# Reordering the opening of a gated cross-attention and mixture-of-experts kernel: shared scales first, first loads from ScalarE, one tile transposed ahead of the first product

## What is computed

```python
def _L0_xattn_ref(x, adj, W, b):            # x: ctx_512, adj: layernorm(x)
    si = jnp.einsum('bnd,d->bn', x, Wi[0])
    sj = jnp.einsum('bnd,d->bn', x, Wj[0])
    xij = jax.nn.sigmoid(si[:, :, None] + sj[:, None, :] + b[0])
    return P_ASEM * xij + (1.0 - P_ASEM) * adj

def _L0_ffn_ref(hidden, ...):               # 16 experts, 4 per token, and a shared one
    probs = jax.nn.softmax(x @ gate_w.T, axis=-1)
    vals, idx = jax.lax.top_k(probs, K)
    ...
    act_s = swiglu(x @ dequant_fp4(shared_gate_up_packed, shared_gate_up_scales))
    out = out + act_s @ dequant_fp4(shared_down_packed, shared_down_scales)

x = x + jnp.tanh(g_xattn[0]) * _L0_xattn_ref(ctx_512, _layernorm(x), W, b)
x = x + jnp.tanh(g_ffn[0]) * _L0_ffn_ref(_layernorm(x), ...)
```

## Time and profile before

| | |
|---|---|
| median of three timed runs | 688.72 us (688.53 to 691.19) |
| profiled execution, its time | 687.41 us |
| profiled execution, its span | 685.6 us |
| busy share PE / DVE / ACT / POOL | 92% / 71% / 47% / 48% |
| granted TensorE clock, mean | 0.982 |
| chain that ended last, PE's share | 80% (DVE 6%, DMA, ACT and POOL 3% each) |
| start of the first gate/up product | 45.4 us |

### The profile page before, as it was taken

The page is one execution under the profiler, slowest core; times in us unless marked ns, Lnnn a source line. Parts: engine busy times, 40 slices in busy tenths (PEclk is TensorE's granted clock), DMA queues, the critical chain, the costliest instruction groups (busy, mean ns, idle before and its releaser), DMA issues.

```text
span 685.6 us, 17258 instructions
## 1 busy us (share of the span) xinstructions
PE 629.7 (92%) x4394; PEld 382.1 (56%) x4395; DVE 488.1 (71%) x1271; ACT 325.3 (47%) x558; POOL 326.2 (48%) x506
## 2 busy tenths in 40 slices
PE   3768969999998999999999999999999999999992
PEld 2444536557554656565665656566565656656561
DVE  6979779895766858588888767778588878767110
ACT  1763567331343455454544554454554545455541
POOL 3621834100334465564646555464655656565432
PEclk9999989999999999999999999999999999999997
DMA  8780101128157875768587594847767587654533
GB/s 234 202 247 2 63 31 64 62 54 276 49 172 160 189 173 127 176 123 195 110 203 176 126 223 74 226 85 201 168 135 183 117 199 158 152 86 77 93 39 39
DMA packets 49841, 93.72 MB, mean 137 GB/s; under 512 B 8840, under 2 KB 16776, under 8 KB 49816
## 3 DMA queue, kind: packets, MB, share of 16 engines
q0 software_dynamic: 16128, 38.35, 30.3%
q1 hardware_dynamic: 32936, 55.04, 27.5%
q10 hardware_dynamic: 752, 0.04, 0.1%
HBM read 65.16 MB, written 28.24 MB: 136 GB/s over the span
## 4 chain that ended last, share of the span: by engine, by line
PE 80%; DVE 6%; DMA 3%; ACT 3%; POOL 3%; issue 2%; SPq 1%; DVEq 0%; POOLq 0%; ACTq 0%
PE gu_ps L1207 45%; PE bank L1235 22%; PE bank L1247 4%; PE bank L1221 4%; DMA dn_sc<-dn_scale_halves 2%; PE bank L1262 1%; DMA room_a<-in_ctx 1%; PE gu_ps L1167 1%; POOL room_a L462 1%; PE bank L1164 1%; PE bank L1191 1%; DVE stats L725 1%; POOL X L445 1%; DVE X L1000 1%; ACT mix_room L581 1%
## 5 line engine op out<-in xcount | busy, mean ns | idle before, releaser
L1207 PE MATMUL gu_ps<-wgu,mix_room 128*128 x1728 | 305.9, 327 | 2.7 <-DVE tick L950 1.6
L1207 PEld LDWEIGHTS gu_ps<-wgu,mix_room 128*128 128x128 f16 x1728 | 166.5, 98 | 114.7 <-issue 7.5
L1235 PE MATMUL bank<-wdn,aT 128*128 (+1 forms) x792 | 186.2, 380 | 3.2 <-ACT aT L629 2.6
L530 POOL DMA_INDIRECT out<-mix_room,idx_s x72 | 122.9, 1707 | 32.4 <-issue 30.9
L629 ACT ACTIVATE aT<-bank 128x768 f16<-128x768 f16 x88 | 71.2, 809 | 139.5 <-PE bank L1221 136.2
L1235 PEld LDWEIGHTS bank<-wdn,aT 128*128 128x128 f16 x792 | 77.6, 98 | 88.8 <-issue 3.6
L501 POOL TENSOR_TENSOR pool_tick<-ones 128x1 f32<-128x1 f32 x144 | 35.7, 248 | 163.6 <-DMA out<-mix_room,idx_s 84.0
L991 DVE SCALAR_TENSOR_TENSOR act<-gu_ps,wslot,sg x72 | 44.5, 618 | 96.4 <-ACT sg L615 84.8
L622 ACT ACTIVATE acth<-act 128x384 f16<-128x384 f32 x88 | 46.0, 523 | 120.1 <-DVE act L991 120.1
L512 POOL DMA_INDIRECT room_b<-token_rows,idx_g x72 | 76.0, 1055 | 12.3 <-issue 3.6
L927 DVE TENSOR_TENSOR wgu<-dq_code,gu_sc 128x768 f16<-128x768 f16 x136 | 72.5, 574 | 2.3
(11 more groups left out here) (157 smaller groups left out, 588.1 us busy)
## 6 DMA issues: line engine op xcount, KB each, us to landing
dn_sc<-dn_scale_halves SPq DMA_DIRECT2D x34, 384.0 KB
dn_raw<-in_L_ffn_down_packed SPq DMA_DIRECT2D x48, 256.0 KB
gu_sc<-gu_scale_halves SPq DMA_DIRECT2D x34, 192.0 KB
X<-in_x SPq DMA_DIRECT2D x4, 1024.0 KB, 8.4
token_rows<-room_a SPq DMA_DIRECT2D x16, 256.0 KB, 2.2
out<-X SPq DMA_DIRECT2D x4, 1024.0 KB, 11.1
gu_raw<-in_L_ffn_gate_up_packed SPq DMA_DIRECT2D x16, 192.0 KB
gu_raw<-in_L_ffn_gate_up_packed SPq DMA_DIRECT2D x16, 191.9 KB
```

The costliest lines, as they stand in the source:

```text
L530: nc.gpsimd.indirect_dma_start(out[:, :], bass.IndirectOffsetOnAxis(idx_s[:, b:b + 1], 0), y_sb[:, b, :], None, compute_op=ALU.add).then_i ...
L1207: mm = nc.tensor.matmul(ps[b][:, 0:I], x(xp * HC + c), wgu[:, w, wp, c, col:col + I], start=(c == 0 and xp == 0 and wp == 0), stop=(c == H ...
L1235: mm = nc.tensor.matmul(y_ps[0 if shared else b][:, :], aT[:, b, ap, t, :], wdn[:, w, wp, t, :], start=(n == 0), stop=(n == 3 * IC - 1))
```

## The change

The split of the scales is done in two parts: the 36 columns of the shared expert first, the 576 of the routed ones after slot 2. ACT issues the contexts and the first X, ahead of and behind the small constants. SP loads the shared scales and the shared packed words first, then the rest. DVE does the gates ahead of `first_stats(0)`, dequantizes the shared gate/up weights from right behind `x_factors(0)` on, and does `first_stats(1)` behind them and `x_factors(1)` behind the first down quarter. PE transposes one tile, not four, ahead of the first product, and tiles 1 to 3 between the products of slots 0 to 2; tile 4 goes behind the second half of slot 3. ACT's copies follow that order. POOL's list is the same as before. The diff's core:

```diff
@@ -144,3 +144,3 @@
         SC_SH, SD_SH = G_GU * GU // P, IC * H // P
-        sc_cut = [0, SC_SH, SC_SH * NE, SC_SH * NE + SD_SH, (SC_SH + SD_SH) * NE]
+        sc_cut = [0, SC_SH, SC_SH + SD_SH, SC_SH * NE + SD_SH, (SC_SH + SD_SH) * NE]
         SCW = sc_cut[-1]
@@ -150,3 +150,3 @@
         sc_rest = sc_room[:, 4 * SCW:6 * SCW].bitcast(F32)
-        sc_h = sc_room[:, 4 * SCW:6 * SCW].rearrange("p (a n) -> p a n", a=2)
+        sc_h = sc_room[:, 6 * SCW:8 * SCW].rearrange("p (a n) -> p a n", a=2)
...
@@ -324,5 +343,7 @@
-        def loaded(n):
+        FIRST_LOADS = 4
-            return 16 * LOADS * (n // 2 + 1)
+        def loaded(n, buf):
+
+            return 16 * LOADS * (n // 2 + 1) - (16 * FIRST_LOADS if buf == 0 else 0)
...
@@ -344,7 +364,4 @@
                 return ap.rearrange("(p n) -> p n", n=sc_cut[k + 1] - sc_cut[k])
-            for k, ap in enumerate((sh_gu_scales.rearrange("g n -> (g n)"), gu_scales.rearrange("e g n -> (e g n)"),
-                                    sh_dn_scales.rearrange("g n -> (g n)"), dn_scales.rearrange("e g n -> (e g n)"))):
-                sp.dma_start(sc_all[:, columns(k)], spread(ap, k)).then_inc(ld_sc, 16)
-            def load_ctx(b):
-                sp.dma_start(ctxs[:, b * TB:(b + 1) * TB, :], ctx_t[b]).then_inc(ld_ctx[b], 16)
+            def load_scale_columns(k, ap, landed):
+                sp.dma_start(sc_all[:, columns(k)], spread(ap, k)).then_inc(landed, 16)
...
-            load_ctx(0)
-            load_x(0)
-            for b in range(1, B):
-                load_ctx(b)
-            load_x(1)
-            sp.wait_ge(vs, SPLIT_STEPS)
-            for part, done in ((0, st_sc_sh), (1, st_sc)):
-                for k, dram in ((part, gu_s_dram), (2 + part, dn_s_dram)):
+            def store_scale_halves(part, done):
...
@@ -364,13 +375,4 @@
                         sp.dma_start(spread(flat, k), sc_h[:, hl, columns(k)]).then_inc(done, 16)
-                if part == 0:
-                    load_words(sp, sh_gu_packed, sh_dn_packed, 0)
-            sp.wait_ge(st_sc_sh, 64)
-            load_scales(sp, 0, 0)
-            sp.wait_ge(ld_w[0], 16 * LOADS)
-            for b in range(2, B):
-                load_x(b)
-            load_words(sp, gu_packed[0], dn_packed[0], 1)
-            sp.wait_ge(st_sc, 64)
-            load_scales(sp, 1, 1)
-            for i in range(NT):
+
...
+            load_scale_columns(0, sh_gu_scales.rearrange("g n -> (g n)"), ld_sc_sh)
+            load_scale_columns(1, sh_dn_scales.rearrange("g n -> (g n)"), ld_sc_sh)
+            load_gate_words(sp, sh_gu_packed, 0, ld_first)
+            sp.wait_ge(split_ready, 1)
+            store_scale_halves(0, st_sc_sh)
+            sp.wait_ge(st_sc_sh, 64)
+            load_gate_scales(sp, 0, 0, ld_first)
+            load_down_words(sp, sh_dn_packed, 0)
+            load_down_scales(sp, 0, 0)
+            load_x(1)
+            load_scale_columns(2, gu_scales.rearrange("e g n -> (e g n)"), ld_sc)
+            load_scale_columns(3, dn_scales.rearrange("e g n -> (e g n)"), ld_sc)
+            for b in range(2, B):
+                load_x(b)
+            load_words(sp, gu_packed[0], dn_packed[0], 1)
+            for i in range(TB):
+                store_rows(i)
+            sp.wait_ge(split_ready, 2)
+            store_scale_halves(1, st_sc)
+            sp.wait_ge(st_sc, 64)
+            load_scales(sp, 1, 1)
+            for i in range(TB, NT):
+                store_rows(i)
...
@@ -549,2 +574,6 @@
         def _(a):
+            def load_ctx(b):
+                a.dma_start(ctxs[:, b * TB:(b + 1) * TB, :], ctx_t[b]).then_inc(ld_ctx[b], 16)
+            load_ctx(0)
+            a.dma_start(X[:, 0:TB, :], x_t[0]).then_inc(ld_x[0], 16)
             for k in range(2):
@@ -556,2 +585,4 @@
             a.dma_start(gws[:, :], gate_w).then_inc(ld_const, 16)
+            for b in range(1, B):
+                load_ctx(b)
@@ -587,7 +618,10 @@
-            for b in range(B - 1):
-                copy_ctxT(b)
+            copy_ctxT(0)
+            copy_ctxT(1)
             scores(0)
-            copy_ctxT(B - 1)
+            copy_ctxT(2)
             scores(1)
+            copy_ctxT(3)
+            scores(2)
+            scores(3)
             for hl in range(2):
@@ -598,9 +632,8 @@
                                      ACT.Copy).then_inc(gwT_ready, 1)
-            scores(2)
-            scores(3)
-            for i in range(TB):
-                high_x(i)
-                if i:
-                    copy_xT(i - 1)
-            copy_xT(TB - 1)
+            high_x(0)
+            high_x(1)
+            copy_xT(0)
+            high_x(2)
+            copy_xT(1)
+            high_x(3)
@@ -648,4 +681,5 @@
-            for i in range(2):
-                activate(i, i)
+            activate(0, 0)
+            copy_xT(2)
+            activate(1, 1)
             copy_aT(0, 0)
@@ -653,2 +687,4 @@
                 copy_aT(i - 1, (i - 1) % 2)
+                if i == 2:
+                    copy_xT(3)
                 if i in WITH_X:
...
-            v.wait_ge(ld_sc, 64)
-            step(nc.vector.tensor_scalar(sc_top, sc_all, SPLITTER, None, ALU.mult))
-            step(nc.vector.tensor_tensor(sc_rest, sc_top, sc_all, ALU.subtract))
...
+            def split_scales(at):
+
+                step(nc.vector.tensor_scalar(sc_top[:, at], sc_all[:, at], SPLITTER, None, ALU.mult))
...
+                nc.vector.scalar_tensor_tensor(sc_h[:, 1, at], sc_all[:, at], W_SCALE, sc_h[:, 0, at], ALU.mult,
+                                               ALU.subtract).then_inc(split_ready, 1)
+            v.wait_ge(ld_sc_sh, 32)
+            split_scales(slice(0, sc_cut[2]))
             v.wait_ge(ld_const, 16 * 6)
@@ -942,3 +981,6 @@
                     v.wait_ge(dqs, n * N_STEPS + 1 - D_STEPS - 1)
-                v.wait_ge(ld_w[buf], loaded(n))
+                if isinstance(n, int) and n == 0:
+                    v.wait_ge(ld_first, 16 * FIRST_LOADS)
+                else:
+                    v.wait_ge(ld_w[buf], loaded(n, buf))
                 words = gu_raw[:, buf, :].bitcast(U16).rearrange("p (n f) -> p n f", f=2)
@@ -968,10 +1010,10 @@
+            split_gates()
             first_stats(0)
             row_scores(0)
-            split_gates()
             x_factors(0)
-            first_stats(1)
+            take_words(0, 0)
+            dequant(0, 0, 0, None)
             row_scores(1)
             attend(0)
-            x_factors(1)
             row_scores(2)
@@ -979,4 +1021,3 @@
             row_scores(3)
-            take_words(0, 0)
-            for k in range(PARTS):
+            for k in range(1, PARTS):
                 dequant(0, 0, k, None)
@@ -984,2 +1025,3 @@
             nc.vector.memset(tick[:, 0:1], 0.0).then_inc(dqg_ready, 1)
+            first_stats(1)
@@ -1005,2 +1047,3 @@
                 if k == 0:
+                    take_words(1, 1)
                     dequant(1, 1, 0, None)
@@ -1035,2 +1078,4 @@
                 if i == 2:
+                    v.wait_ge(ld_sc, 32)
+                    split_scales(slice(sc_cut[2], SCW))
                     first_stats(2)
@@ -1073,2 +1118,3 @@
+            v.wait_ge(ld_w[0], loaded(0, 0))
             for d in range(PARTS):
@@ -1076,2 +1122,4 @@
                     dequant(0, 0, None, d)
+                    if d == 0:
+                        x_factors(1)
                 else:
@@ -1082,3 +1130,2 @@
             nc.vector.memset(tick[:, 0:1], 0.0).then_inc(dq_ready, 1)
-            take_words(1, 1)
             attend(1)
@@ -1168,3 +1215,2 @@
             transpose_ctx(0)
-            transpose_ctx(1)
             pe.wait_ge(wj_ready, 1)
@@ -1172,7 +1218,5 @@
             score_parts(0)
-            transpose_ctx(2)
-            score_parts(1)
-            transpose_ctx(3)
-            score_parts(2)
-            score_parts(3)
+            for b in range(1, B):
+                transpose_ctx(b)
+                score_parts(b)
@@ -1266,2 +1310,4 @@
             def shared_gate_up(i, half):
+                if half == 0:
+                    pe.wait_ge(xT_ready, i + 1)
                 gate_up(i, i % 2, lambda k: xT[:, i, k // HC, k % HC, :], 0, half)
@@ -1270,12 +1316,13 @@
             pe.wait_ge(si_ready, B)
-            for i in range(TB):
-                transpose_x(i)
-                if i:
-                    route(i - 1)
+            transpose_x(0)
             pe.wait_ge(sig_ready, NT)
             pe.wait_ge(dqg_ready, 1)
-            for i in range(2):
-                for half in range(2):
-                    shared_gate_up(i, half)
-            route(TB - 1)
+            shared_gate_up(0, 0)
+            transpose_x(1)
+            route(0)
+            shared_gate_up(0, 1)
+            shared_gate_up(1, 0)
+            transpose_x(2)
+            route(1)
+            shared_gate_up(1, 1)
             transpose_act(0, 0)
@@ -1290,5 +1337,8 @@
                 transpose_act(i - 1, 1 - b)
-                if i in WITH_X:
```

(8 more changed lines are left out.)

29 lines of the change are left out of this document (20 added, 9 removed).

## The result

The changed kernel takes 705.14 us (median of 4 runs, 705.09 to 709.09) against 689.69 us (688.53 to 691.19, 4 runs) of the kernel before on the same chip: a ratio of 1.0237 with a 95% interval of 1.0194 to 1.028. The forecast was 699.3 with a range of 694.5 to 703.5. The sign and the chain of causes were right; the size was some 6 us short, and the measured time lies 1.6 us above the upper end of the range. Between the two medians lie 15.5 us.

What follows compares the result with a forecast made beforehand. Bound: PE, through its first product at 45.44 and 10.3 us idle after it. Delays of 7.5 (first product), 9.8 (gate), 9.3 (attend(1)), then 10.6 (tile 8): 687.4 + 10.6 = 698.0, plus 1.3 gives 699.3 us; range 694.5 to 703.5.

Steps and rivals of the forecast that it cites:

- rival (a): Between first product and tile 8, products put ahead of transposes hand back about 4 us: 695.3 us; chance 0.14.
- (c): Stores of rows 4 to 7 come later than high_x(8) needs them, some 4 us more: 703.3 us; chance 0.04.
- some 10: Behind the 576-column split: some 10 us for issues and landing of its halves, ahead of a 4.8 us load, all hidden.
- loads ahead of the first dequantization: SyncE's packed words and shared scales in the opening: cost nothing, hidden by 7 us of DVE work.
- first product, put at 2.4 us: First 12 matmuls on PE, ahead of the first gate: 2.4 us, half of 4.80.
- the same steps as before: First gate to attend(1): unchanged except take_words(1,1) moved to slot 5, 0.5 us back, so the delay is 9.3 us.
- a split of 3.3 us: DVE's 576-column split in slot 2: 3.3 us, 2.0 of it in idle time, so 1.3 added and 10.6 in all.
- the list products, put at nothing: PE's list products behind tile 8: no further delay, 10.6 us there as at tile 8.
- 2.0 us set for sharing with POOL's scaled_x: DVE's part 0 of the first dequantization, slowed beside POOL's four scaled_x: 2.0 us, with 0 to 3 as bounds.
- Rival (b): In the opening, constants or shared scales come late, at the upper bound of 12.5: 3 us more, 702.3 us; chance 0.15.
- Rival (d): POOL's second group does not hold up the first tile; first product at 36.7, run ends near 683 us; chance 0.04.
- The outer sum: Slow end: constants at 12.5, all 3.0 us lost beside scaled_x, and the low clock (up to 1.5 us): 704.8 us.

Runs made afterwards that it cites:

- pool_order: Changed kernel with only POOL's list reordered, group 0's second norm and low_x(0) to low_x(2) ahead of group 1's inverse_std: 689.31 us, ratio 1.0006.
- stats_ahead: Changed kernel with first_stats(1) and x_factors(1) moved on DVE ahead of parts 1 to 3 of the first dequantization: 697.58 us, ratio 1.0108.
- warm2: Changed kernel with 270 identity transposes added on PE in its idle time ahead of tile 0: 703.1 us, ratio 1.0204.
- list_dense: Changed kernel with one identity transpose behind each of the 62 list matmuls not last in their block: 703.5 us, ratio 1.0225.
- the experiment on the list products: Both kernels profiled again unchanged (707.45 and 690.72 us), and both with transposes put between list matmuls (703.5 and 689.87 us).
- warm: Changed kernel with 320 identity transposes added on PE in its idle time ahead of tile 0: 702.86 us, ratio 1.0197.

## Why the prediction was right in sign and short in size

**What held.** The bound, the order of the chain, and what each wait of it up to the first gate ended on. PE sets the pace from tile 8 on, so what delays tile 8 goes into the end. POOL's order decides the first product (53.92 for a forecast of 53.0, pool_order and stats_ahead from both sides). The first gate hangs on ACT with the table load right ahead of it (60.49, then 61.78). Between gate and tile 8 nothing is handed back on balance (46.4 us for 42.2), so rival (a) is out, and high_x(8) did not wait for its row, so (c) is out. dqg_ready came at 37.67 for 36.5, x_factors(1) ended at 43.1 for 42.2. The "some 10" for the issues and the landing of the split halves was too much: behind the second split the loads were issued 3.0 us after the first store (85.31 to 88.30), so that this way was hidden with more to spare than said.

**What failed, in short.** Not the order of events but the terms of the sum. The loads ahead of the first dequantization, put at nothing, cost a wait of 2.73 us. The first product, put at 2.4 us, took 3.63 at the low clock. The way from attend(1) to tile 8, put at "the same steps as before" and a split of 3.3 us, had a slow down product and a split of 5.76 us beside POOL. And the list products, put at nothing, ran 3.7 us longer at a lower clock.

**What failed, in the order of the sum.** The forecast said 10.6 us; the span shows 17.7. The 7.1 us between them are these terms:

1. Loads costed at nothing. "I cost its loads at nothing, hidden by the 7 us of DVE work" was wrong: take_words(0,0) waits 2.73 us for gu_sc, whose load took 6.8 us from its issue at 13.23. The 2.0 us set for sharing with POOL's scaled_x were then not needed, since that had ended by 20.45; with x_factors(0) 0.6 late (the constants at 10.27 for 9.55, as late as in the second profile of the kernel before) part 0 ended 1.5 late, dqg_ready 1.2 and the first product 0.9. That the first product came so near its forecast is therefore in part luck: 2.73 us of waiting that were not in the sum and 2.0 us of sharing that were in it and not needed. The prediction named 1 to 3 us "without that cover"; the cover was there on paper, 7 us, and was too short.
2. The first twelve matmuls taken at 2.4 us, "half of 4.80", from a row in which PE had been at work and the clock was 1.00. They took 3.63: 1.2 us. With item 1 that is 2.1; the steps behind it gave 0.4 back (tile 1's transposes took 0.5 for the 0.8 put down), so that the gate is 1.7 late against the forecast. The clock was left out of the sum although the change took 7.9 us of PE work out of the opening and so gave PE the 20.8 us of idle time behind which the clock was low.
3. "attend(1) follows by the same steps as before ... nothing is handed back" held for attend(1) (11.1 against 9.3, all of it carried over), but not for the slots behind it: from there to low(2) 2.1 us more were lost, where the first down product ran 3.04 us and DVE waited 0.68 and 0.72 us for products and 0.57 for an activation. warm2, with these products at full clock, takes 1.7 of it back. Since list_dense has them at full clock without a fill, this loss may belong to the execution and not to the change; both profiles of the changed kernel show it.
4. The split costed at 3.3 us, "3.5 times 576/612", from a row with nothing beside it. In slot 2 it took 5.76 beside POOL's low_x: 2.5 us more. Where it met one low_x less, as in warm, warm2 and list_dense, it took 4.9. The prediction knew this price: it charged it to part 0 beside scaled_x and forgot it here. Since the later waits gave 3.3 us back instead of 2.0, the net of this step is 1.2 above the forecast.
5. From tile 8 on the forecast had nothing. 1.2 us came back until the list products, 3.7 were lost among them to the clock, 0.5 came back behind: 2.0. As the experiment on the list products shows, these 3.7 may belong to the execution and not to the change.

Items 1 to 4 are 5.1 us at tile 8 (1.8 up to attend(1), then 2.1 and 1.2), item 5 is 2.0.

**The rivals.** Rival (b) came true in part: the scales were late, the constants only by 0.7. Rival (d) was put at 683 if POOL let the first tile through. pool_order is that case and gives 689.3: the first product came at 40.19 and not at 36.7, because low_x and the dequantization then share the time, and most of the gain went to the low clock of the first products, to ACT's longer way to the gate (8.6 us from the first product on, 4.8 before) and to the split. That rival's price counted no low clock and no sharing between low_x and the dequantization. Its condition, x_factors(1) ended by 34.6, was also not enough by itself: in stats_ahead it ends at 34.59, but the weights then come at 45.27 and the copy of the first tile ends at 47.0, and the first product is at 47.16.

**The range.** The outer sum behind it allowed 1.5 us for one product at the lower clock. The first half product (1.2), the first down product (0.9 over 2.1) and the list blocks (3.7) each took a share, and the split beside POOL had no upper bound of its own, although held the price: 0.84 us for each low_x met.

## To carry to other kernels

When a change brings one engine's work forward, read the lists of the engines that feed the same consumer: here DVE's weights came 5 us earlier and the first tile's low_x 14.7 us later, because POOL's list, which the diff does not touch, had been written for the old order of DVE. Work that is put into an idle gap still has a price: it takes the port, the DMA engines or the engine of a neighbour, so cost it from a row where the neighbour is at work, not from one where it stood alone. And idle time on TensorE can be paid a second time, in the clock of the products that follow: behind 20.8 us of it the first twelve matmuls took 3.63 us for 2.11, while behind some 3 us the first down product took 2.10 in some executions and 2.8 to 3.7 in others.

## What was not expected of the hardware

- A block that keeps PE busy all the time can still lose the full clock: 32 matmuls of 80 columns in 5.25 us were followed by products at 4.02 us, and a transpose of 128 columns between them held it at 2.13.
- The first instruction of the 36-column split took 1.43 us, the next of the same width 0.20; POOL's iota of 1.60 us (slot_place) ran beside it from 3.73.
- 288 KB more ahead on one queue delayed transfers of a few KB on another by 2.6 to 3.7 us (constants at 12.85 and 14.00 for 10.27).
- With the same lists on every engine, the way from the first gate to tile 8 took 43.8 us in one execution and 46.4 in others; the difference went with the clock of the first down product (2.10 us, or 3.04 to 3.21).
- Two profiles of the same kernel differed by 1.4 us in the list stretch alone, more than what separates any of the five variants with POOL's list mended from the next in time (at most 1.2).
